# Graph convolution, gather stage: lane numbers and a mask read from PSUM, three accumulation banks, adds three groups behind

## The reference

```python
h = x @ W
deg = jax.ops.segment_sum(jnp.ones_like(dst, dtype=h.dtype), dst, num_segments=N)
deg_inv_sqrt = jnp.where(deg > 0, jax.lax.rsqrt(jnp.maximum(deg, 1)), 0.0)
norm = deg_inv_sqrt[src] * deg_inv_sqrt[dst]
msgs = h[src] * norm[:, None]
out = jax.ops.segment_sum(msgs, dst, num_segments=N)
```

## Time and profile before

| | us |
|---|---|
| median of 3 runs | 2717.07 (2711.66 to 2721.03) |
| the profiled execution | 2699.77 |
| its span in the trace | 2698.0 |
| front, to 136 us | 136 |
| gather stage, 136 to 1290 us | 1154 |
| the stages behind it | 1408 |

### The profile page before, as it was taken

The page is one execution under the profiler, slowest core; times in us unless marked ns, Lnnn a source line. Parts: engine busy times, 40 slices in busy tenths (PEclk is TensorE's granted clock), DMA queues, the critical chain, the costliest instruction groups (busy, mean ns, idle before and its releaser), DMA issues. The chain is left out here.

```text
span 2698.0 us, 47112 instructions
## 1 busy us (share of the span) xinstructions
PE 2235.2 (83%) x12457; PEld 1841.6 (68%) x12458; DVE 1444.8 (54%) x4035; ACT 833.2 (31%) x2320; POOL 1615.6 (60%) x2085
## 2 busy tenths in 40 slices
PE   7876777777666775555879999999998999996998
PEld 5744555555555554443869999977777999995898
DVE  9754443434444454333862222239997888887211
ACT  2511222221111111111523333325663444442333
POOL 5676666666666677666025555547776777771233
PEclk9987777877778787776579999999999999997999
DMA  5233333332333333333313434323221111111122
GB/s 161 99 98 88 87 89 90 89 88 84 89 91 92 89 92 92 90 93 90 108 49 121 123 113 138 122 67 117 86 85 52 47 49 49 47 47 63 30 36 31
DMA packets 139023, 227.28 MB, mean 84 GB/s; under 512 B 26923, under 2 KB 99456, under 8 KB 138946
## 3 DMA queue, kind: packets, MB, share of 16 engines
q0 software_dynamic: 56240, 142.70, 19.2%
q1 hardware_dynamic: 81186, 82.10, 9.1%
q10 hardware_dynamic: 1520, 1.58, 0.2%
HBM read 174.97 MB, written 51.30 MB: 84 GB/s over the span
## 5 line engine op out<-in xcount | busy, mean ns | idle before, releaser
L945 POOL DMA_INDIRECT all_XN<-h_table,l_srcI x782 | 776.5, 993 | 369.0 <-issue 216.7
L1152 PE MATMUL gcn_acc<-all_XN,gcn_hot 128*128 128x256 f32 x796 | 264.5, 489 | 100.3 <-DVE all_X L1037 58.2
L1152 PE MATMUL gcn_acc<-all_XN 128*128 128x256 f32 x768 | 247.9, 479 | 103.0 <-DMA all_XN<-h_table,l_srcI 47.4
L1152 PEld LDWEIGHTS gcn_acc<-all_XN,gcn_hot 128*128 128x128 f32 x796 | 186.4, 245 | 161.9 <-DVE all_X L1037 79.0
L1152 PEld LDWEIGHTS gcn_acc<-all_XN 128*128 128x128 f32 x768 | 176.7, 241 | 157.4 <-issue 71.5
L879 ACT COPY gcn_seen_sb<-gcn_seen 128x392 f32<-128x392 f32 x98 | 47.4, 484 | 595.3 <-remote 441.9
L1858 ACT ACTIVATE moe_hidden<-moe_hid_ps,moe_b 128x128 f32<-128x128 f32 x420 | 131.1, 363 | 277.7 <-PE moe_hid_ps L1939 255.6
L1037 DVE SCALAR_TENSOR_TENSOR all_X<-gcn_acc,all_XN,all_X 128x256 f32 x392 | 170.8, 475 | 77.4 <-remote 60.5
L1939 PEld LDWEIGHTS moe_hid_ps<-moe_xst,held_held 128*128 128x128 f32 x1680 | 202.8, 192 | 10.6 <-issue 6.0
L1045 DVE COPY_PREDICATED gcn_last_seen<-gcn_seen_sb,gcn_seen 128x392 f32<-128x392 int32 x98 | 57.6, 588 | 280.8 <-issue 148.0
L1939 PE MATMUL moe_hid_ps<-moe_xst,held_held 128*128 128x128 f32 x1680 | 206.1, 276 | 0.6 <-DVE moe_xst L1879 0.6
(11 more groups left out here) (440 smaller groups left out, 4635.5 us busy)
## 6 DMA issues: line engine op xcount, KB each, us to landing
held_held<-in_e_w SPq DMA_DIRECT2D x32, 512.0 KB
slots_out<-moe_y SPq DMA_DIRECT2D x105, 128.0 KB
all_XN<-h_table,l_srcI POOLq DMA_INDIRECT x782
all_X<-in_x SPq DMA_DIRECT2D x7, 896.0 KB, 11.0
rows_table<-all_XN SPq DMA_DIRECT2D x7, 896.0 KB, 4.2
z_table<-held_held SPq DMA_DIRECT2D x49, 128.0 KB
x_table<-all_XN SPq DMA_DIRECT2D x49, 128.0 KB, 1.7
out<-all_X SPq DMA_DIRECT2D x49, 128.0 KB, 1.7
```

Of the source, the lines that this page charges most:

```text
L945: nc.gpsimd.indirect_dma_start(msg[b][:, c, :], None, self.h_table, bass.IndirectOffsetOnAxis(self.srcI[:, GE * g + c:GE * g + c + 1], 0)) ...
L1152: last = nc.tensor.matmul(acc[b % NA][:, :], hot[b % NH][:, c, :], msg[b][:, c, :], start=(c == 0), stop=(c == n - 1))
```

## The change

Four things. The 128 lane numbers are copied once into a PSUM bank of their own, `numbers`, and `targets` compares with them there. The second masked copy takes its mask from `seen` in PSUM (its bits read as int32) in place of the SBUF copy. To make room for `numbers`, `acc` has 3 banks instead of 4: `BANK` gives each b its bank, and `APART` says how many groups back the bank was last used, which is what PE waits for. And DVE adds 3 groups behind instead of 4.

```diff
-        NA = 4
+        NA = 3
+        BANK = (0, 1, 2, 0, 1, 2, 0, 1)
+        APART = (2, 2, 5, 3, 3, 3, 3, 3)
-        LAG = 4
+        LAG = 3
@@ banks
             acc = s.banks("acc", NA, D)
+            numbers = s.bank("numbers", P)
@@ DVE
+                    nc.vector.tensor_copy(numbers[:, :], self.iota[:, :]).then_inc(numbers_ready, 1)
@@ targets
                         nc.vector.tensor_tensor(hot[b % NH][:, :, :], self.dst_lo[:, ds(GE * g, GE)].unsqueeze(2).broadcast_to([P, GE, P]),
-                                                self.iota[:, :].unsqueeze(1).broadcast_to([P, GE, P]), ALU.is_equal).then_inc(hot_ready, 1)
+                                                numbers[:, :].unsqueeze(1).broadcast_to([P, GE, P]), ALU.is_equal).then_inc(hot_ready, 1)
@@ add_up
-                            nc.vector.scalar_tensor_tensor(x, acc[b % NA][:, :], scale[:, k, ds(g, 1)], x, ALU.mult, ALU.add).then_inc(added, 1)
+                            nc.vector.scalar_tensor_tensor(x, acc[BANK[b]][:, :], scale[:, k, ds(g, 1)], x, ALU.mult, ALU.add).then_inc(added, 1)
@@ last_edges
-                        nc.vector.copy_predicated(last_tile[:, :], seen_sb[k % 2][:, :], tile_no[k % 2][:, :]).then_inc(lasts_kept, 1)
+                        nc.vector.copy_predicated(last_tile[:, :], seen[k % NP][:, :].bitcast(I32), tile_no[k % 2][:, :]).then_inc(lasts_kept, 1)
@@ sum_up (PE)
-                        after(pe, added, 2 * (g - NA + 1))
+                        after(pe, added, 2 * (g - APART[b] + 1))
                         for c in range(n):
-                            last = nc.tensor.matmul(acc[b % NA][:, :], hot[b % NH][:, c, :], msg[b][:, c, :], start=(c == 0), stop=(c == n - 1))
+                            last = nc.tensor.matmul(acc[BANK[b]][:, :], hot[b % NH][:, c, :], msg[b][:, c, :], start=(c == 0), stop=(c == n - 1))
```

More of the change, by code:

```diff
@@ L784, in gather_stage @@
             acc = s.banks("acc", NA, D)
+            numbers = s.bank("numbers", P)
+            numbers_ready = s.sem("numbers_ready")
             seen = s.banks("seen", NP, PT * T)
@@ L1010, in _ @@
                     cols = [None]
+                    dve.wait_ge(numbers_ready, 1)
                     def columns(g, b, q):
```

## The result

The changed kernel takes 2748.07 us (median of 4 runs, 2740.51 to 2753.64) where the kernel before takes 2718.03 beside it: a ratio of 1.0113, with a 95% interval of 1.0083 to 1.0144. It is 1.1% slower. A point of the ratio's third decimal is 2.7 us.

What follows compares the result with a forecast made beforehand. POOL's wait for late news of PE's sums was taken to set the gather stage's pace. 2699.77 - 3.6 + 0.3 + 0 = 2696.5 us for the profiled execution, carried over to the median as 2714; range 2688 to 2750.

Steps and rivals of the forecast that it cites:

- Stretches: POOL's gathers held up by DVE instructions with two SBUF inputs: 28 us of POOL's time would go.
- A tenth of it reaches the end: POOL's long waits in the gather stage absorb most of the removed stretches; 28 x 0.13 = 3.6 us gained.
- rival A: In the gather stage the stretches come off the end in full: 28 us, 2689; chance 0.28, in whole or by half.
- Pace by POOL's wait for PE's news: In all three parts of the gather stage, late news of PE's sums sets the pace, near 5.8 us a group.
- DVE's durations: One-hots and second masked copy with a PSUM operand: +2 ns taken for the one-hots, hidden in DVE's idle time.
- The copy: Copying the numbers into PSUM once, ahead of the first one-hots: 0.3 us added on the path.
- Three banks and a lag of three: PE's extra waits for DVE's adds, followed through the last loop, stay hidden: 0 us, bounds -8 and +69.
- PE has less to spare: Beside keys, values and attention, PE's extra waits have less cover: bounds -8 and +69 us, taken 0.
- Rival B: PE's earlier waits at b = 0 and 1 delay POOL: +34 us (2748) once a turn, +69 (2783) twice; chance 0.25.
- the forecast's own mechanism: In the gather stage stretches are absorbed and PE's waits hidden: 2704 to 2722 by its own bounds; chance 0.44.

Runs made afterwards that it cites:

- e15: Changed kernel (three banks, lag of three) with compare numbers and second copy's mask both read from SBUF, e2 again on another chip: 1.0067 of the kernel before.
- e6: Changed kernel with the second copy's mask read from SBUF again, compare numbers still in PSUM: 1.005 of the kernel before.
- e5: The changed kernel itself, both operands in PSUM, timed again on another chip: 1.0111 of the kernel before.
- e7: Changed kernel with compare numbers back in SBUF, only the second copy's mask in PSUM: 1.0132 of the kernel before.
- e4: Kernel before with POOL asking for the sum of five groups back instead of four: 1.001 of the kernel before.
- e17: Kernel before with a lag of three, four banks and SBUF operands, PE made to wait for adds as three banks would demand: 1.0051 of the kernel before.
- e8: Changed kernel with DVE's adds of groups b = 6 and 7 moved one turn earlier: 1.0056 of the kernel before.
- e3: Kernel before with the second copy's mask from PSUM, and compare numbers in a free PSUM bank from group 144 on: 0.9985 of the kernel before.
- e2: Changed kernel with both operands back in SBUF, three banks and lag of three kept: 1.004 of the kernel before.
- e16: Three banks, lag of three, numbers in SBUF, mask in PSUM everywhere, the kernel of e7 on another chip: 1.0108 of the kernel before.
- e10: e8 (early adds) with the second copy's mask read from SBUF, compare numbers still in PSUM: 1.0015 of the kernel before.
- e18: e17 (four banks, waits as with three) with the second copy's mask read from PSUM: 1.0074 of the kernel before.
- e9: e1 (four banks, lag of three) with the second copy's mask read from PSUM: 1.0 of the kernel before.
- e1: Kernel before with only the lag cut from four to three, four banks and SBUF operands kept: 0.9983 of the kernel before.
- e12: e2 with the second copy's mask in PSUM only in the loop beside the attention: 1.0066 of the kernel before.
- e13: e2 with the second copy's mask in PSUM only in the loop beside keys and values: 1.0079 of the kernel before.
- e14: e2 with the second copy's mask in PSUM only in the last loop, from group 144 on: 1.0071 of the kernel before.

## Why the prediction was wrong, and where it was right

Steps by the prediction's numbers.

1. **Stretches, right.** 28 us forecast, 26.3 measured; the mean 0.959 where 0.957 was named. They are the operand's doing: in e15, with both operands in SBUF, 56 of 60 gathers that start in the one-hots are stretched (over 1.00 us) and 30 of 38 in the second masked copy; in e6, with the numbers alone in PSUM, 0 of 67 and 33 of 50.
2. **A tenth of it reaches the end, right in kind.** With the numbers in PSUM and not, e5 and e7 on one chip have 1.0111 and 1.0132 with overlapping intervals, e6 and e15 on two 1.005 and 1.0067: 0.2% less at most, where rival A wanted 0.9% (24.9 us). The 3.6 us are too small to be seen. Idle time took up the whole of it: 17.2 us more against 15.8 less of work in e6. The factor itself stood on little: in the trace before, a line through the 22 spans of three groups from 17.2 to 17.7 us has 0.12, one through the 19 from 17.3 has 0.06.
3. **Pace by POOL's wait for PE's news.** The last part came to 5.84 us a group (300.9/51.5) from 5.73. The spans of three groups did not stay at 17.4: they had a mean of 18.17 (17.6 without the one of 28.7), and spans of two groups rose from 7 to 28. e4 shows that the lead isn't what is short. Why the news comes late stays unexplained, as it was.
4. **DVE's durations.** +2 ns forecast, -9 measured (680 for 689). Nothing hangs on it. By the rule of the Trainium skill, "VectorE: DVE Perf Modes", on the TRN2 errata, the one-hots would take 65 ns longer with a PSUM operand, an estimate; the trace has them 9 ns shorter.
5. **The copy.** Within anything measured.
6. **Three banks and a lag of three, taken at 0: this step failed.** Its result held for the loop it was taken from. There PE's sum of b = 1 was to start 10.7 us later, behind masked copies that wait for ACT's copy, and be hidden. The changed kernel has twelve waits of 9 us for adds in the last part (107.7 us), with 5.9 us more for the part. Six stand ahead of b = 4, five of b = 0 and none of b = 1, but they are of that kind. One reading in the working was wrong and changes nothing: PE was not without work from 1093 to 1100.77, it summed group 162 from 1093.27 to 1096.68 and had 4.09 us idle. At 1106 us in the changed kernel (PE's sum of group 156, b = 4): ACT's copy and POOL's gather are released together, DVE works through to the add, and PE starts after 11.04 us, with POOL 0.30 us between its gathers all the while:

```profile
1106.21 0.49 ACT L883 COPY gcn_seen_sb<-gcn_seen 128x392 f32<-128x392 f32 x1 [16.22 <-remote]
1106.46 0.95 POOL L949 DMA_INDIRECT all_XN<-h_table,l_srcI  x1 [3.16 <-remote]
...
1109.42 0.87 DVE L1043 SCALAR_TENSOR_TENSOR all_X<-gcn_acc,all_XN,all_X 128x256 f32 x2
...
1110.21 0.95 POOL L949 DMA_INDIRECT all_XN<-h_table,l_srcI  x1 [0.30 <-issue]
1110.34 5.42 PE L1158 MATMUL gcn_acc<-all_XN 128*128 128x256 f32 x16 [11.04 <-DVE all_X L1043]
```

But the result was carried over to the other two loops with one sentence, "PE has less to spare", which was a bound and no working. Followed through the attention's turn in the same way, it would have met L1063 in DVE's queue between PE's product and the add of b = 7, a cycle that the last loop does not have. e17 (+16 us there) and e8 (-27 us there) show that this is it. A second term was put at nothing without a reason: that reading the mask from PSUM might cost anything but DVE's own time. It goes with 0.4 to 0.6% of the whole.

**Rival B** gave 2748 and the mechanism: earlier waits of PE, idle over 400 us, waits for L1043 ahead of b = 0 and 1. All of that came. Its size was right by luck, as a sum of other parts: it had 1.56 us in each of 22 turns, and the trace has some 3 us in each of the 8 turns beside the attention (25 us), about 7 at the start of that loop, where the longest wait grew from 7.1 to 14.0 us, and little in the last. Those 7 can't be put down to the waits: e3, with four banks and the old lag, has 15.4 us at that place and e15, with three banks, 7.2. Its place was named as both b = 0 and 1 of every loop; it was b = 1 of one loop. And by e2, e15 and e17 the waits bring only about 14 us. The rest, 0.4 to 0.7%, came in with the mask, which no step and no rival had. That the range reached up to 2750 was this rival's doing; the forecast's own mechanism allowed 2722.

**Open: the mask.** The one edit between the kernels of e15 and e16 is where the second masked copy's mask is read: no wait and no order in the code changes, and its mean duration goes from 585 to 581 ns. With three banks the kernel with the mask in PSUM is slower in every pair: by 0.61% (e5 to e6, one chip), 0.41 (e16 to e15, one chip, intervals that just overlap) and 0.41 (e8 to e10, two chips). With four banks it is 0.23 (e18 to e17) and 0.17 (e9 to e1), intervals overlapping, and e3, which has that mask, lies 0.15% under the kernel before. The profiled executions don't show the time: the stage's gathers end at 1317 to 1323 us in six of the seven that have three banks, the adds where the change put them and the mask in one place throughout, three with the mask in PSUM and three without, and at 1332 in the seventh (e16).

One thing in the traces does go with the mask. Beside the attention PE's wait ahead of b = 7, where it needs b = 4 added, sums over the eight turns to 57 to 79 us in the five runs that have the mask in PSUM in that loop (after, e5, e7, e12, e16) and to 20 to 30 us in the five that don't (e2, e6, e13, e14, e15); the wait ahead of the next b = 0 is shorter in return, 12 to 22 against 27 to 46 us. With four banks and the same waits it is 49 us with the mask in PSUM (e18) and 25 without (e17). In turn 15 of the changed kernel and of e15:

```profile
891.13 3.78 PE L1158 MATMUL gcn_acc<-all_XN 128*128 128x256 f32 x8 [8.30 <-DVE all_X L1043]
```
```profile
931.15 3.78 PE L1154 MATMUL gcn_acc<-all_XN 128*128 128x256 f32 x8 [4.10 <-DVE all_X L1039]
```

That part took 399 to 410 us in the five (mean 404.6) and 394 to 404 in the others (398.8), one execution each: some 6 us, half of what the ratios say or less, and e12, whose mask is in PSUM in this loop alone, has the ratio of e15. So this is a trace of the mask and not its price. Why the wait is longer isn't known.

## What to carry to other kernels

Follow a new wait through each loop in which it stands, with everything that lies ahead of its release in the other engine's queue: waits for adds were almost free in the loop with twelve times 9 us of them, and eight of 3.6 us cost 16 to 25 us in the loop where the add stood behind an addition that itself waited for the waiting engine. Where an engine's work is freed but its pace comes from another's sums, the freed time turns into idle time; 15.8 us of gathers did so here (e15 to e6). And to tell a resource from the waits it brings, keep the resource and add the waits, as e17 did with two lines: it came out at 1.0051, between the two timings of the kernel that really gave the bank up.

## What the runs showed of the hardware

A gather that starts on POOL beside an instruction of DVE is often held up by one that reads two tensors from SBUF, and in no case here by one that has a tensor in PSUM in place of one of them. Of the gathers that start in the one-hots, 56 of 60 last over 1.00 us in e15 and 0 of 67 in e6; the gather's mean fell from 995 to 975 ns with that alone. The one-hots themselves (512 elements) take 681 ns in e6 where e15 has 685 to 687.

The eight sums of b = 1 beside the attention that start after 3.60 to 3.66 us of waiting take 3.78 us each (granted clock 0.50 at 855.50 us of the changed kernel). In e8 the same eight follow on other work and take 1.99 (1.00 at 838.89 us). So an added wait costs PE more than its own length: here 1.8 us on top of 3.6.

With three banks, a read of the mask from PSUM instead of SBUF by one of DVE's copies, 98 times, goes with 0.4 to 0.6% more of the whole, without a trace in its own duration (581 for 585 ns); with four banks the runs can't tell it from nothing (-0.15 to +0.23%).

POOL's lead doesn't set the stage's pace: four or five groups ahead, about 5.75 us a group in the last loop (5.741 before, 5.757 in e4).
